# Stack of batch 1 by selection products, maxima of batch 0 by a small product, and a new order, in a fused attention and mixture-of-experts kernel

## The reference

```python
def _L0_attn_ref(x, w_qkv, w_out):            # 16 batches, 256 tokens, 128 features
    qkv = jnp.einsum('bnc,ce->bne', x, w_qkv)
    q, k, v = jnp.split(qkv, 3, axis=-1)
    to_heads = lambda t: t.reshape(b, n, h, d).transpose(0, 2, 1, 3)   # h = 16, d = 8
    q, k, v = (to_heads(q), to_heads(k), to_heads(v))
    attn = jnp.einsum('bhnd,bhmd->bhnm', q, k) / scale
    attn = jax.nn.softmax(attn, axis=-1)
    out = jnp.einsum('bhnm,bhmd->bhnd', attn, v)
    return jnp.einsum('bnc,co->bno', out.transpose(0, 2, 1, 3).reshape(b, n, c), w_out)

def _L0_ffn_ref(x, Wr, Wg, Wu, Wd, Sg, Su, Sd, expert_bias):
    logits = xf @ Wr + expert_bias
    top_v, top_i = jax.lax.top_k(logits, K)   # E = 8 experts, K = 2
    ...
    h = jax.nn.silu(gate) * up
    eo = jnp.einsum('tef,efd->ted', h, Wd)
    out = jnp.einsum('te,ted->td', rw, eo)
    return out + jax.nn.silu(xf @ Sg) * (xf @ Su) @ Sd

x = x + _layernorm(_L0_attn_ref(_layernorm(x), w_qkv, w_out))
x = x + _layernorm(_L0_ffn_ref(_layernorm(x), ...))
```

## Time and profile before

| what | value |
|---|---|
| median of 3 runs | 373.18 us (371.95 to 376.94) |
| the profiled execution | 371.26 us, of it 369.5 us span from the first to the last instruction |
| TensorE busy | 350.6 us, 95% of the span |
| VectorE busy | 313.2 us, 85% |
| ScalarE busy | 267.3 us, 72% |
| GpSimd busy | 200.5 us, 54% |
| mean granted TensorE clock | 0.996 of full speed |

### The profile page before, as it was taken

How to read it: one execution, slowest core, us unless ns; L and a number is a source line. 1 busy time by engine, 2 the same in 40 slices (tenths; PEclk the granted TensorE clock), 3 DMA queues, 4 the chain that set the end, 5 groups by cost and what they waited for, 6 DMA issues and landing times.

```text
span 369.5 us, 10052 instructions
## 1 busy us (share of the span) xinstructions
PE 350.6 (95%) x3304; PEld 227.0 (61%) x3304; DVE 313.2 (85%) x788; ACT 267.3 (72%) x511; POOL 200.5 (54%) x518
## 2 busy tenths in 40 slices
PE   8998999999999989999999999999999999998892
PEld 7856555544665546575757475666765556667772
DVE  8796698989999996999897899999999986768661
ACT  4752688699788876969886797788768868864522
POOL 7333053324663544777565465755763576767654
PEclk9999999999999999999999999999999999999998
DMA  2266988554665574266456455487265041322211
GB/s 84 67 148 139 208 168 179 142 116 128 163 178 104 153 152 139 75 132 163 132 170 166 128 117 149 129 187 166 81 185 142 19 130 33 116 64 71 56 34 31
DMA packets 59922, 45.65 MB, mean 124 GB/s; under 512 B 8966, under 2 KB 56966, under 8 KB 59870
## 3 DMA queue, kind: packets, MB, share of 16 engines
q1 hardware_dynamic: 59870, 45.00, 48.5%
HBM read 26.69 MB, written 17.81 MB: 120 GB/s over the span
## 4 chain that ended last, share of the span: by engine, by line
PE 60%; issue 10%; POOL 10%; DVE 9%; ACT 4%; DMA 3%; SPq 2%; POOLq 0%; DVEq 0%; ACTq 0%
PE pvp L661 12%; PE bank_d L831 8%; PE bank_d L815 8%; PE sc L645 8%; PE sc L629 6%; PE bank_d L816 5%; DVE mx L1010 4%; PE bank_a L714 3%; POOL rstd L1152 2%; POOL hidden L1219 2%; PE bank_d L668 2%; DMA ks<-qk_dram 2%; POOL parts L1163 2%; DVE rden L1042 1%; PE bank_d L806 1%
## 5 line engine op out<-in xcount | busy, mean ns | idle before, releaser
L1010 DVE TENSOR_REDUCE mx<-sc 128x4 f32<-128x1024 f32 x128 | 154.2, 1217 | 18.5 <-PE sc L629 17.7
L859 ACT ACTIVATE pr<-sc 128x1024 f32<-128x1024 f32 x128 | 130.7, 1024 | 27.2 <-PE sc L645 26.4
L661 PE MATMUL pvp<-pr,va 128*32 128x256 f32 x1024 | 68.5, 385 | 0.0
L815 PE MATMUL bank_d<-x3T,wg_sb 128*128 128x256 f32 x160 | 54.3, 421 | 2.4 <-DVE hidden L1108 2.0
L645 PE MATMUL sc<-qs,ks 51*128 51x256 bf16 x512 | 49.6, 274 | 1.8 <-DMA qs<-mT 0.9
L629 PE MATMUL sc<-ks,qs 48*128 48x256 bf16 x512 | 49.6, 272 | 1.8 <-DVE mx L1010 1.1
L1219 POOL TENSOR_TENSOR hidden<-hidden,rwb 128x256 f32<-128x256 f32 x60 | 42.3, 729 | 12.6 <-DMA rwb<-rw_dram 11.8
L816 PE MATMUL bank_d<-x3T,wu_sb 128*128 128x256 f32 x160 | 47.6, 379 | 0.0
L1152 POOL TENSOR_TENSOR rstd<-vareps,mhalf 128x2 f32<-128x2 f32 x64 | 44.5, 696 | 0.0
L661 PEld LDWEIGHTS pvp<-pr,va 128*32 128x32 f32 x1024 | 26.7, 109 | 25.1 <-issue 12.4
L831 PE MATMUL bank_d<-wd_sb,hidden 128*128 128x128 f32 x320 | 39.4, 278 | 2.2 <-POOL hidden L1219 2.2
(11 more groups left out here) (115 smaller groups left out, 506.8 us busy)
## 6 DMA issues: line engine op xcount, KB each, us to landing
rwb<-rw_dram SPq DMA_DIRECT2D x30, 256.0 KB, 4.2
qk_dram<-parts SPq DMA_DIRECT2D x30, 192.0 KB, 2.7
qs<-qk_dram SPq DMA_DIRECT2D x30, 192.0 KB, 4.1
ks<-qk_dram SPq DMA_DIRECT2D x30, 192.0 KB, 4.9
qk_dram<-parts SPq DMA_DIRECT2D x30, 128.0 KB, 2.6
pv_dram<-pv_sb SPq DMA_DIRECT2D x14, 256.0 KB, 2.2
x_sb<-in_L_attn_x_dram SPq DMA_DIRECT2D x16, 128.0 KB, 2.7
out_dram<-x SPq DMA_DIRECT2D x16, 128.0 KB, 1.8
```

Of the source, the lines that this page charges most:

```text
L661: mm = pe.matmul(pvp[32 * j:32 * j + 32, g, :], values[:, X * c + 4 * g + j, 32 * tt:32 * tt + 32], pr[:, k, c * N:(c + 1) * N], start=(tt ...
L815: pe.matmul(bank_d[bank][:, 0:N], wg_sb[:, ORDER[n], :], x3T[b % 2][:], start=True, stop=True)
L859: nc.scalar.activation(pr[:, 2 * s:2 * s + 2, :].rearrange("p k n -> p (k n)"), sc[PAIR["s2", b, s]][:].rearrange("p u c n -> p (u c n)"), ...
L1010: nc.vector.tensor_reduce(mx[b % 2][:, :, :, s].rearrange("p c u -> p u c"), sc[PAIR["s1", b, s]][:], AX.X, ALU.max).then_inc(max_done, 1)
```

## The change

The stack of batch 1 is made on TensorE too. Eight new steps `u0` to `u7` compute it two pairs of heads at a time, for k and q in turn (6 products each, in the half bank `bank_d[0]` or in `pvp`), and eight copies on ScalarE, `uc0` to `uc7`, bring it to `ks` and `qs`. Batch 1 has no `spill` and no `stack` any more; `s1_0`, `s1_2`, `s1_4` and `s1_6` of batch 1 wait for the copies that they need.

The maxima of batch 0 are no longer put into the stack by DMA. `maxT` of batch 0 writes them to rows 0 to 23 and 64 to 87 with four products in place of two, `max_copy` is two copies in place of one, and each `s2` step of batch 0 adds four products of 24 rows to its four of 48: a column of a new matrix `msel` with -1 in three rows, repeated 128 times, times `mT`. GpSimd builds `msel` with a memset and six `affine_select` instructions. `load_minus` moves from before the maxima of batch 0 are taken to after all eight copies.

The identity products go from 75 to 52, at other places (again 17 before the first transpose, `FILL_LAST` unchanged). The whole table `TIMES` is a new one, so steps of all batches stand in another order.

```diff
-    "w_load": [403, 612, 725, ...
+    "w_load": [406, 589, 745, ...
-    "down": [451, 659, 789, ...
+    "down": [458, 668, 798, ...
...
 FILL = {
-    "maxT": {0: 9, 2: 1}, "qk": {0: 2}, "s1_2": {0: 1, 1: 1}, "s1_3": {1: 1}, "s1_6": {2: 3, 3: 2}, "s2_3": {1: 4},
-    "s2_4": {0: 3}, "s2_5": {0: 4}, "sel1": {0: 3}, "xT": {0: 17, 3: 4, 5: 1},
+    "maxT": {0: 3}, "qk": {0: 3}, "s1_3": {1: 1}, "s1_6": {3: 1}, "s2_0": {0: 4}, "s2_1": {0: 1, 1: 3}, "s2_2": {0: 1},
+    "s2_3": {1: 2}, "s2_4": {1: 1}, "s2_5": {0: 3}, "s2_6": {1: 1}, "sel1": {0: 4}, "selq": {0: 2}, "v": {1: 1, 5: 2},
+    "xT": {0: 17, 6: 2},
 }
 FILL_SCORES = {
-    ("s1", 0, 2): 1,
-    ("s1", 0, 3): 1,
-    ("s1", 1, 0): 5,
...
 }
...
+                if b >= 2 and s == 0:
+                    pe.wait_ge(qk_stacked[b % 2], landed2(4, b))
+                if b == 1 and s % 2 == 0:
+                    pe.wait_ge(unit_copied, s + 2)
...
-                        rows = slice(64 * u, 64 * u + ROWS_MAX)
-                        mm = pe.matmul(sc[pair][:, u, c, :], k[rows, s, c * P:(c + 1) * P], q[rows, s, :], start=True, stop=True)
+                        rows = slice(64 * u, 64 * u + (ROWS_MAX if b else ROWS))
+                        mm = pe.matmul(sc[pair][:, u, c, :], k[rows, s, c * P:(c + 1) * P], q[rows, s, :], start=True, stop=b > 0)
+                    if b == 0:
+                        for u in range(2):
+                            rows = slice(64 * u, 64 * u + 3 * X)
+                            mm = pe.matmul(sc[pair][:, u, c, :], msel[rows, s:s + 1].broadcast_to([3 * X, P]), mT[0][rows], start=False, stop=True)
...
+                for j in range(8):
+                    if due(tick, f"u{j}") is not None:
+                        pe.wait_ge(part3_done, 2)
+                        if j < 2:
+                            pe.wait_ge(qh_copied, 2)
+                        else:
+                            pe.wait_ge(unit_copied, j - 1)
+                        bank = bank_d[0][0:WIDTH].rearrange("p (x n) -> p x n", x=2) if j % 2 == 0 else pvp[0:WIDTH]
+                        q = 1 - j % 2
+                        for x in range(2):
+                            for n in range(3):
+                                mm = pe.matmul(bank[:, x, :], lay[:, n, q, 2 * (j // 2) + x, :], parts[1][:, q, n, :], start=(n == 0), stop=(n == 2))
+                        mm.then_inc(unit_done, 1)
...
+                for j in range(8):
+                    if due(tick, f"uc{j}") is not None:
+                        act.wait_ge(unit_done, j + 1)
+                        bank = bank_d[0][0:WIDTH].rearrange("p (x n) -> p x n", x=2) if j % 2 == 0 else pvp[0:WIDTH]
+                        dst = qs[1][0:WIDTH] if j % 2 else ks[0:WIDTH, 1]
+                        nc.scalar.copy(dst[:, 2 * (j // 2):2 * (j // 2) + 2, :], bank).then_inc(unit_copied, 1)
```

More of the change, by code:

```diff
@@ L51 @@
[L51 to L60, removed]
@@ L65 @@
+    "xT": [27, 50, 67, 118, 139, 211, 275, 385, 488, 614, 756, 862, 988, 1096, 1204, 1332],
+    "lay0a": [29],
+    "xT_copy": [30, 53, 69, 121, 142, 213, 276, 390, 491, 619, 766, 867, 998, 1102, 1208, 1347],
+    "lay2": [32],
+    "load_wout": [33],
[9 rows of a table added]
+    "v_copy": [48, 76, 109, 148, 200, 272, 366, 513, 590, 698, 839, 941, 1065, 1191, 1324, 1437],
+    "sel3": [52],
+    "msel": [55],
+    "load_wd": [57],
     "ql_copy": [59],
     "kh_copy": [60],
-    "selq": [62],
-    "kl_copy": [63],
[4 rows of a table removed]
-    "spill": [None, 74, 123, 143, 193, 253, 341, 455, 576, 680, 830, 947, 1018, 1165, 1258, 1403],
@@ new lines @@
+    "spill": [None, None, 131, 162, 209, 281, 329, 472, 595, 678, 811, 944, 1049, 1167, 1264, 1403],
+    "maxT": [135, 186, 252, 313, 402, 522, 628, 717, 850, 958, 1072, 1218, 1305, 1450, 1531, 1651],
+    "max_copy": [136, 189, 255, 318, 408, 525, 645, 732, 854, 969, 1076, 1221, 1313, 1452, 1534, 1653],
[4 rows of a table added]
+    "stack": [None, None, 145, 201, 234, 300, 460, 502, 625, 707, 869, 983, 1105, 1256, 1311, 1465],
+    "s2_2": [149, 217, 298, 365, 466, 568, 700, 795, 916, 1043, 1144, 1277, 1393, 1496, 1600, 1695],
@@ L191 @@
-    "s2_4": {0: 3}, "s2_5": {0: 4}, "sel1": {0: 3}, "xT": {0: 17, 3: 4, 5: 1},
+    "maxT": {0: 3},
+    "qk": {0: 3},
+    "s1_3": {1: 1},
+    "s1_6": {3: 1},
+    "s2_0": {0: 4},
+    "s2_1": {0: 1, 1: 3},
+    "s2_2": {0: 1},
+    "s2_3": {1: 2},
+    "s2_4": {1: 1},
+    "s2_5": {0: 3},
+    "s2_6": {1: 1},
+    "sel1": {0: 4},
+    "selq": {0: 2},
+    "v": {1: 1, 5: 2},
+    "xT": {0: 17, 6: 2},
 }
 FILL_SCORES = {
-    ("s1", 0, 2): 1,
-    ("s1", 0, 3): 1,
-    ("s1", 1, 0): 5,
-    ("s1", 1, 3): 1,
@@ L242, in landed1, with landed2 @@
         return DMA * n * ((b + 1) // 2)
+    def landed2(n, b):
+        return DMA * n * (b // 2)
     LAST = NB - 1
@@ L296, in sandwich @@
         mrest = ring(2, "mrest", [P, TT, 2, X])
-        mT = ring(2, "mT", [3 * H, N], BF16)
+        mT = ring(2, "mT", [64 + 3 * X, N], BF16)
+        msel = sb("msel", [64 + 3 * X, X], BF16)
         pr = sb("pr", [P, H, TT * N])
@@ L1172, in _ @@
                     nc.gpsimd.memset(minus[:], -1.0).then_inc(minus_done, 1)
+                if due(tick, "msel") is not None:
+                    nc.gpsimd.memset(msel[:], 0.0).then_inc(msel_zeroed, 1)
+                    pool.wait_ge(msel_zeroed, 1)
+                    for n in range(6):
+                        first = 64 * (n // 3) + X * (n % 3)
+                        nc.gpsimd.affine_select(out=msel[:], in_=msel[:], compare_op=ALU.not_equal, fill=-1.0, base=-first,
+                                                pattern=[[-1, X]], channel_multiplier=1).then_inc(msel_done, 1)
+                        pool.wait_ge(msel_done, n + 1)
                 if (b := due(tick, "msplit")) is not None:
```

208 lines of the change are left out of this document (124 added, 84 removed), and 144 rows, old and new, of the table TIMES.

## The result

The changed kernel takes 378.11 us (median of 19, 374.33 to 382.48) beside 372.03 us for the kernel before (median of 19): a ratio of **1.013, with an interval from 1.0107 to 1.0154**. It is slower, and the median lies above the whole predicted range. The ratio leaves out the four slow executions of the 19 (380.94 us and more), without which the median is 376.64 us, so the loss is 4.8 us by the ratio and 6.1 us by the medians of all. The profiled execution took 381.31 us, 3.2 us over the median; TensorE's clock was at half in two stretches of it.

The account below looks back on a forecast made before the run. TensorE's queue was taken to set the time (busy 350.6 of 369.5 us). Queue +0.5 and waits -3.2 gave -2.7 us: 368.6 us for the profiled execution, 370.5 us for the median, range 366.0 to 376.8.

Parts of the forecast that it names:

- the third term of the sum: TensorE's queue: four more 24-row products in each of batch 0's eight `s2` steps, +1.8 us, with +4.7 as other end.
- Rival 2: Batch 0's small products change the tile shape: +2.9 us on the forecast, 373.4 us; chance 0.12.
- from 140 on the order is new but of the same density: Waits of TensorE after 140 us: taken as 0, with 1.5 us to either side.
- rival 1: New order closes the 2.15 us wait and opens others as large: 373.7 us; chance 0.27, shared with no effect.
- the third rival: Start to 52 us: identity products stood in waits that stay, 381.2 us, or 377.2 with half; chance 0.07.
- Identity products 23 fewer: TensorE's queue: 75 to 52 identity products at 0.326 us each, -7.5 us.
- `u` steps 0.75 each: TensorE's queue: eight new steps of six products, 0.75 us each, +6.0 us.
- Waits of the start: TensorE from 17.38 to 35.79 us: -0.6 us; idle from 17 to 52 us forecast under 2 us.
- First `s2` of batch 0: Sign: it starts at about 34 to 36 us, with four `s1` steps of batch 1 done before it.
- `down` of batch 1 without a wait: Sign between 120 and 140 us: TensorE no longer waits there for GpSimd's products with the routing weights.
- the -2.1 of my sum: Waits, 120 to 140 us: all of the 2.15 us wait at `down` of batch 1 taken as gain, -2.1 us.
- 80 to 120 us, -0.5: Waits: half of TensorE's 1.04 us there goes, as VectorE comes with less idle time behind it, -0.5 us.

Follow-up runs that it names:

- pad48: Changed kernel with batch 0's small products made over 48 rows in place of 24, the added rows zeros: 373.38 us, ratio 1.005.
- again: The changed kernel once more, unedited: 377.46 us, ratio 1.017.
- rwfree: Three kernels (before, changed, pad48) with the routing weights left out of batches 2 to 15: 368.65, 371.40 and 367.76 us.
- oldstart: Kernel before, its old order up to tick 205 and the new order behind, without `u` steps or small products: 376.82 us, ratio 1.0115.
- rwfree_pad48: pad48 with GpSimd's products of batches 2 to 15 taken with a tile already in place, not the loaded routing weights: 367.76 us, ratio 0.990.
- queue: pad48 with SyncE's queue reordered in six batches, spills or loads of the routing weights moved earlier: 377.48 us, ratio 1.018.
- queue2: queue without three of its moves (load of batch 2, spills of batches 10 and 11): 371.61 us, ratio 1.0033.
- rwfree_after: Changed kernel with GpSimd's products of batches 2 to 15 taken with a tile already in place, not the loaded routing weights: 371.40 us, ratio 1.0004.
- rwfree_before: Kernel before with GpSimd's products of batches 2 to 15 taken with a tile already in place, not the loaded routing weights: 368.65 us, ratio 0.9926.
- newstart: Changed kernel with its new order up to tick 225 and the old order behind: 379.35 us, ratio 1.0236.
- before_queue: Kernel before with batch 1's routing weights spill and load put ahead of batch 8's spill in SyncE's queue: 371.27 us, ratio 1.0005.

## Why the prediction was wrong

**The step that failed first** is the third term of the sum, "between 1.8 and 4.7 I take 1.8". The eight steps grew by 0.86 - 0.32 = 0.54 us each, 4.3 us, close to the other end. pad48 shows the cause; the whole price, with the clock falls that hang on it, was 4.1 us. Rival 2 was right on this term (its 373.4 us was not what came) and my reason against it was wrong: that 51 and 48 rows follow each other freely says nothing of 24. It had a chance of 0.12, with one row for it, and no row against it that bore on 24 rows; the Trainium skill's rule should have moved it ahead.

**The second** is "from 140 on the order is new but of the same density; I take 0, with 1.5 us to either side". The same paths were there, but nearer to TensorE: 10.06 us of waits in the new stretch against 2.30, 7.8 us more, where my range had 1.5. Even with the 2.15 us gone, TensorE waits 4.5 us more from the first `down` to the last (*again*). rwfree sizes the routing weights' share: 5.6 to 6.7 us against 2.6, so about +3 to +4 us (+2 to +3.5 by the ratios). That is rival 1, the hole that moves, at about twice the size I gave it, for I had priced only the 2.15 us that would come back.

**A third** was said to have no term, and has one: the clock. I wrote that it stayed whole through 2.15 us of wait. It did, and then fell after two waits of 0.4 us. In four traces (changed kernel, *again*, oldstart, rwfree_pad48) the clock falls at 72 to 76 us, at the second of the two waits of 0.4 us or right behind it; pad48, queue, queue2 and rwfree_after have the same two waits and no fall there. Behind 2.15 us the clock stayed whole, behind 2.02 (pad48) and 1.94 (rwfree_before) it fell. Half clock lasts 3.4 us in most of them, a cost of 1.7 us, but 6.9 in queue and newstart and 10.3 in rwfree_before. What decides whether it comes wasn't settled. It is part of why the new kernel's executions spread over 8 us.

Point by point for the rest:

- The rivals were priced one at a time. Two of them came together, and their own prices give 370.5 + 3.2 + 2.9 = 376.6 us; the clock is on top. No chance was given to that. The range's upper end, 376.8, also leaves out the half of the third rival (377.2) that it says it takes in.
- "Identity products in 31 of the 58" between 17.38 and 35.79: the order has 26 there, and the trace 53 passes. Nothing else hangs on it.
- Identity products 23 fewer, `u` steps 0.75 each (measured 0.77), `maxT`: as forecast.
- Waits of the start: right, and better. From 17.38 to 52.50 us TensorE waits for nothing (I had said under 2 us); rival 3, waits that stay, is out. The copies `uc` and the step `msel` cost nothing that shows.
- First `s2` of batch 0 "at 34 to 36 us": 34.38.
- `down` of batch 1 without a wait: right. But before_queue shows that this place was worth nothing by itself (0.2 us, inside the interval), so that the -2.1 of my sum was wrong although its wait went. It was read off one execution, and the only other trace of the same program up to there hasn't got the wait.
- 80 to 120 us, -0.5: 0.73 us of wait against 1.04, in a stretch that has also moved by some 3 us; right in sign, small.
- The sum without both causes, rwfree_pad48 beside rwfree_before, is -0.9 us. The forecast without its -2.1 was -0.6; that they are so close is luck in part, since the intervals of the two runs reach 1.0 and 1.4 us to either side. So the account: -0.9, +3.6 to +4.1 for the tile shape, +3 for the routing weights' path, 5.7 to 6.2 us together. That this meets the measured 6.1 us is no check, since the terms are differences of the same runs and must close. What the runs do show is that the shape's price is nearly the same with the path (4.1) and without it (3.6), so the two causes add. The clock falls are inside these terms and not a fourth one.

Open: which move of the new order brought the weights' path nearer. Cuts at a tick couldn't tell, since each seam makes waits of its own, and queue and queue2 don't show that SyncE's queue holds any of it beyond the noise.

## What to carry to other kernels

A small matrix product that uses fewer rows than its neighbours can cost more than one padded with zeros to their shape: where a trace shows any step at a change of shape, price each new shape as a change until a row says otherwise. A wait seen at a nearly full engine is seldom worth its length, and may be one of that execution only: take it away and ask which path comes next, how far behind it is, and who is now queued behind the DMA that was moved. In a shared DMA queue a small transfer that the busiest engine needs goes ahead of a large one (the runs here put 1.9 us on it in one place), and a DMA whose source isn't ready yet doesn't go ahead of anything.

## What the runs showed of the hardware that was not expected

VectorE was held up beside a memset of GpSimd. Before, four copies of 32 elements take 2.05 us beside a memset of 1.85 us (first VectorE's row, then GpSimd's):

```profile
6.62 2.05 DVE L980 COPY wv_sb<-wqkv_sb 128x32 f32<-128x32 f32 x4
```

```profile
6.76 1.85 POOL L1172 MEMSET minus<- 4x2048 bf16 x1
```

After, the memset stands elsewhere (28.3 us) and takes 1.79 us, and the same four copies take 0.43 us. So it is VectorE that waited:

```profile
6.83 0.43 DVE L1059 COPY wv_sb<-wqkv_sb 128x32 f32<-128x32 f32 x4
```

The Trainium skill, SBUF — State Buffer, section Who interferes with whom, says that a VectorE instruction in a two-port mode and one of GpSimd exclude each other for the length of the first; the times fit, though no run tried it alone.

The start differs by execution. pad48 and rwfree_pad48 begin with the same program, but the 34 passes of identity products that nothing holds up take 5.61 us in one and 6.90 in the other, and everything behind them is moved by 1.3 us (first `s2` at 33.52 and 34.81). The passes go at one pace first and at nearly twice that pace later, and only the time of the change differs (about 4.8 and 7.5 us). That looks like the two levels of the clock, but the granted clock of the profile reads 1.00 all the while, so the clock is not shown to be the cause.
